# A transformer block: ScalarE takes over the copy of the k and q products, and TensorE sums the eighth key tile

## The chip, the cores and the metric

The kernel runs on one core of a Trainium2 chip. TensorE multiplies matrices, VectorE (DVE), ScalarE (ACT) and GpSimd (POOL) work on tiles element by element, SyncE (SP) issues transfers. Matmul results land in PSUM, which is divided into banks of 128 partitions by 512 fp32 elements. The metric is the device time of one execution in microseconds (us): 1811.17 us as the median of three runs of the kernel before (1810.55 to 1813.67).

## The reference

One block with conditioning, for 4 sequences of 1024 rows of 512 features, 16 heads of 32:

```python
ada = jax.nn.silu(c) @ Wada.T + bada
shift_msa, scale_msa, gate_msa, shift_mlp, scale_mlp, gate_mlp = jnp.split(ada, 6, axis=-1)
h = modulate(rmsnorm(x, g1, D), scale_msa, shift_msa)
qkv = h @ Wqkv.T + bqkv                       # -> q, k, v by head
q = rmsnorm(q, gq, hd) * hd ** (-0.5)
k = rmsnorm(k, gk, hd)
attn = jax.nn.softmax(jnp.einsum('bhqd,bhkd->bhqk', q, k), axis=-1)
o = jnp.einsum('bhqk,bhkd->bhqd', attn, v)    # -> rows of 512
x = x + gate_msa[:, None, :] * (o @ Wproj.T + bproj)
h = modulate(rmsnorm(x, g2, D), scale_mlp, shift_mlp)
x = x + gate_mlp[:, None, :] * (gelu(h @ Wfc1.T + bfc1) @ Wfc2.T + bfc2)
```

## The kernel before

The work has two parts: attention (to 977 us in the trace) and then the MLP. The change touches attention only.

**Steps.** Attention is written out as steps L = -25 to 255, and every engine has its own list of instructions in which step follows step. A step from 0 on treats one tile of 128 keys against 512 queries for a group of four heads. Eight steps (key tiles j = 0 to 7) make one half-group hh, of which there are 32; 16 steps make a group, 64 a batch b. In step L:

- TensorE (qk, L513) multiplies keys by queries into two scores banks p = 0 and 1, each holding two heads.
- ScalarE (exponentials, L704) makes two exponentials of 128x1024 from them into one of three probs buffers.
- VectorE (add, L791) adds the probs of the step before to sums, seven adds of 128x2048 for eight key tiles, since the first add takes two of them.
- TensorE (weigh, L530) multiplies probs by v. Up to step 207 it does so in odd steps for two steps at once; from then on (PAIRED = 207) one step at a time.
- One step behind the eighth key tile, TensorE sums sums over the 128 partitions (row_sums, L547: four matmuls side by side, one for each head, into the bank aux), ScalarE moves the result (move_rows, L713), and by way of DRAM its inverse comes back as a factor for the output (o_out, L801).

**Products.** Between qk(L, 0), qk(L, 1) and weigh, TensorE fills in the projections of later groups and batches: a table, PLAN, gives each product its steps (one, two or three), and six or four matmuls go into each step, half of them after qk(L, 0) and half after qk(L, 1) (fill). A product of 12 matmuls gives k or q for four heads and 512 rows (L588, called a unit) or v for 128 rows (L601). All products from step 0 on use a single bank, gemm: the first matmul of a product waits until the product before it has been moved out (bank_free). The last product ends in step 207.

**What a unit goes through.** VectorE moves it out with the bias added, into one of two raw buffers (raw_out, L816), in the step after its last. ScalarE squares it (L674), TensorE sums the squares by head into aux (sum_squares, L554), ScalarE takes the logarithm (L664) and from it, a half step later, the inverse root by an exponential (L668), both in the one buffer norms. VectorE multiplies (L862, called normalising below), splits the result into a high and a low part (L871, L873: together make_parts), and SyncE stores them to DRAM and loads them as k_stack and q_stack. The tables RAW_AT, SUM_AT, INV_AT and FIN_AT give the steps of raw_out and square, of sum_squares, of the logarithm and root, and of make_parts. SUM_AT is two steps behind the unit's end, and later where another sum, a row sum or a turn has that step; INV_AT and FIN_AT are one and two steps behind it. The logarithm of unit n waits for normalising of unit n-1 (normed) and stands ahead of its step's exponentials in ScalarE's list.

**The x tiles.** A tile of 128 rows of x for a later batch is loaded to one of three xt buffers, summed in squares (L834) and normalised (L842) by VectorE, turned by TensorE into aux (turn, L565), scaled on VectorE (L855) and split by ScalarE (L695) and GpSimd. The table TURN gives the steps, each eighth step from 50 on.

```python
RAW_AT = {step + 1: n for n, step in enumerate(UNIT_END)}
    step += 1 if step < 0 else 2                       # SUM_AT
            parts_first = L in FIN_AT and (L < 0 or L in RAW_AT and RAW_AT[L] == FIN_AT[L] + 2)
```

## Time and profile before

| | us |
|---|---|
| median of three runs | 1811.17 |
| the profiled execution's own time | 1810.62 |
| its span in the trace | 1808.8 |
| TensorE busy (matmul) | 1727.9 |
| VectorE busy | 1085.6 |
| ScalarE busy | 919.6 |
| exponentials of attention (L704), 512 | 548.7 |
| adds to sums (L791), 192 of 224 | 453.8 |
| load of an x tile, issue to landing | 3.1 |

The profile is of one execution. A busy TensorE isn't TensorE at its peak: matmuls overlap, and the ends of matmuls in the trace are modelled, so that one of 0.39 us is followed by the next 0.23 us after its start. The bracket at the end of a row is the time that the engine was idle ahead of the instruction, and what released it. Two instructions of one kind in a row are merged (x2), and a row sum of four fp32 matmuls shows as eight records. PEclk is the granted clock of TensorE as a share of 2.4 GHz.

### The profile page before, as it was taken

How to read it: one execution, taken by the hardware profiler on the slowest of the kernel's cores; microseconds unless marked ns; L12 is line 12 of the kernel's file. 1: busy time of each engine (PE TensorE's matmuls, PEld its weight loads, DVE VectorE, ACT ScalarE, POOL GpSimd, SP SyncE). 2: the span in 40 equal slices, each digit the busy share in tenths (PEclk: the TensorE clock that was granted, in tenths of full speed). 3: DMA queues.
4: the chain of work that ended last, by engine and by line, in shares of the span. 5: the costliest groups of instructions: out<-in, count | busy, mean ns of one | idle time of the engine just before them, and what ended most of it. 6: DMA issues, size and time to landing. Idle time of an engine off the chain costs nothing.

```text
span 1808.8 us, 23247 instructions
## 1 busy us (share of the span) xinstructions
PE 1727.9 (96%) x8376; PEld 1154.5 (64%) x8376; DVE 1085.6 (60%) x1325; ACT 919.6 (51%) x1136; POOL 372.5 (21%) x305
## 2 busy tenths in 40 slices
PE   6998999999999999999889999999999999999998
PEld 3554555555555555554224787878788887878786
DVE  6678888898898898878788545142332324142301
ACT  4476666777777777778787432222221212221221
POOL 3001111100001000000140233333332333333332
PEclk8999999999999999999999899999999999999999
DMA  5754545555555555555765201010020202010000
GB/s 195 214 144 132 135 123 139 132 147 135 154 135 134 146 130 156 127 135 153 174 144 196 74 18 58 25 52 24 12 70 6 64 17 64 17 52 23 17 18 24
DMA packets 122242, 176.92 MB, mean 98 GB/s; under 512 B 29568, under 2 KB 43904, under 8 KB 121136
## 3 DMA queue, kind: packets, MB, share of 16 engines
q1 hardware_dynamic: 115952, 156.41, 32.3%
q10 hardware_dynamic: 5408, 16.81, 2.5%
q0 software_dynamic: 800, 2.62, 0.5%
q8 instruction: 50, 0.82, 0.2%
q14 instruction: 32, 0.26, 0.1%
HBM read 124.87 MB, written 50.92 MB: 97 GB/s over the span
## 4 chain that ended last, share of the span: by engine, by line
PE 44%; issue 29%; DVE 11%; POOL 9%; ACT 4%; DMA 2%; SPq 0%; POOLq 0%; ACTq 0%; DVEq 0%
PE scores L513 9%; PE pv L530 8%; PE gemm L588 7%; DVE sums L791 5%; PE scores L1303 5%; POOL act_parts L1235 5%; PE gemm L601 4%; ACT probs L704 3%; PE pv L1320 3%; PE gemm L1320 2%; PE aux L554 2%; POOL y L1233 2%; PE aux L547 1%; DVE raw L816 1%; DVE raw L862 1%
## 5 line engine op out<-in xcount | busy, mean ns | idle before, releaser
L704 ACT ACTIVATE probs<-scores,shift 128x1024 f32<-128x1024 f32 x512 | 548.7, 1113 | 195.4 <-PE scores L513 178.7
L791 DVE TENSOR_TENSOR sums<-sums,probs 128x2048 f32<-128x2048 f32 x192 | 453.8, 2363 | 32.7 <-ACT probs L704 28.0
L513 PE MATMUL scores<-q_stack,k_stack 128*128 128x512 f32 x1024 | 358.8, 435 | 6.3 <-ACT probs L704 6.1
L1303 PE MATMUL scores<-w_hi,act_parts 128*128 128x512 f32 x1024 | 318.7, 392 | 0.0
L513 PEld LDWEIGHTS scores<-q_stack,k_stack 128*128 128x128 f32 x1024 | 173.8, 189 | 202.3 <-issue 105.5
L1235 POOL TENSOR_TENSOR act_parts<-act_full,act_parts 128x512 fp32r<-128x512 f32 x128 | 172.5, 1348 | 514.2 <-ACT act_parts L1166 513.6
L530 PE MATMUL pv<-probs,v 128*32 128x512 f32 x2048 | 253.1, 603 | 0.4 <-ACT probs L704 0.4
L1303 PEld LDWEIGHTS scores<-w_hi,act_parts 128*128 128x128 f32 x1024 | 191.4, 189 | 38.8
L1303 PE MATMUL scores<-w_lo,act_parts 128*128 128x512 f32 x512 | 199.9, 391 | 0.0
L1373 DVE TENSOR_TENSOR y_next<-pv,p_bias 128x512 f32<-128x512 f32 x28 | 19.3, 691 | 299.7 <-PE pv L1275 299.7
L1166 ACT ACTIVATE act_parts<-act_full 128x512 fp32r<-128x512 f32 x128 | 80.9, 632 | 224.5 <-PE scores L1303 223.5
L1320 PE MATMUL gemm<-z,w 128*128 128x512 f32 x768 | 186.9, 393 | 2.6 <-DVE z L1478 2.6
L1320 PE MATMUL pv<-z,w 128*128 128x512 f32 x768 | 185.4, 390 | 0.0
L1320 PEld LDWEIGHTS gemm<-z,w 128*128 128x128 f32 x768 | 145.7, 190 | 33.4 <-DVE z L1478 3.0
L1320 PEld LDWEIGHTS pv<-z,w 128*128 128x128 f32 x768 | 143.7, 188 | 29.8
L530 PEld LDWEIGHTS pv<-probs,v 128*32 128x32 f32 x2048 | 54.3, 110 | 133.7 <-issue 103.5
L1154 ACT ACTIVATE act_full<-gemm,f_bias 128x512 f32<-128x512 f32 x64 | 44.2, 690 | 186.4 <-PE gemm L1320 179.9
L588 PE MATMUL gemm<-h_hi,wq_hi 128*128 128x512 f32 x248 | 101.9, 411 | 22.8 <-DVE raw L816 18.9
L1154 ACT ACTIVATE act_full<-pv,f_bias 128x512 f32<-128x512 f32 x64 | 44.0, 688 | 149.2 <-PE pv L1320 147.8
L765 POOL TENSOR_TENSOR x_inv<-x_sqc,minus_half 128x1 f32<-128x1 f32 x32 | 17.6, 550 | 450.0 <-DVE x_sqc L837 450.0
L1303 PEld LDWEIGHTS scores<-w_lo,act_parts 128*128 128x128 f32 x512 | 96.6, 189 | 20.4
L588 PE MATMUL gemm<-h_hi,wq_lo 128*128 128x512 f32 x248 | 99.0, 399 | 0.0
(167 smaller groups left out, 1944.1 us busy)
## 6 DMA issues: line engine op xcount, KB each, us to landing
k_stack<-parts_scratch SPq DMA_DIRECT2D x128, 256.0 KB, 5.0
q_stack<-parts_scratch SPq DMA_DIRECT2D x128, 256.0 KB, 5.1
parts_scratch<-parts SPq DMA_DIRECT2D x62, 512.0 KB, 2.9
inverse<-inverse_scratch SPq DMA_DIRECT2D x128, 64.0 KB, 2.1
heads_out<-o_out SPq DMA_DIRECT2D x32, 256.0 KB, 5.2
out<-result SPq DMA_DIRECT2D x32, 256.0 KB, 2.0
heads<-heads_out SPq DMA_DIRECT2D x28, 256.0 KB, 3.6
x_tile<-in_x SPq DMA_DIRECT2D x28, 256.0 KB, 2.8
```

Of the source, the lines that this page charges most:

```text
L513: mm = nc.tensor.matmul(scores[p][:, i, :], k_stack[s][:, h, j * P:(j + 1) * P], q_stack[half][:, h, :], start=True, stop=True)
L530: mm = nc.tensor.matmul(pv[hh % NH][h * DH:(h + 1) * DH, :], v[b % 2][:, j, (g * HG + h) * DH:(g * HG + h + 1) * DH], probs[l % RING][:, h ...
L554: nc.tensor.matmul(aux[:], small["head_ones"][:], squares[:], start=True, stop=True).then_inc(ss_mm, 1)
L588: mm = nc.tensor.matmul(bank_of_product(p)[:], w[:, k, at:at + P], h[:, k, c], start=(n == 0), stop=(n == len(terms) - 1))
L601: mm = nc.tensor.matmul(bank_of_product(p)[:], h[:, k, c], w[:, k, 2 * D:3 * D], start=(n == 0), stop=(n == len(terms) - 1))
L704: nc.scalar.activation(probs[L % RING][:, 2 * p:2 * p + 2, :], scores[p][:], ACT.Exp, bias=small["shift"][:]).then_inc(exp_done, 1)
L791: nc.vector.tensor_tensor(sums[:], a[:], probs[l % RING][:], ALU.add).then_inc(added, 1)
L1154: nc.scalar.activation(act_full[m % 2][:], up[m % 2], ACT.Gelu_apprx_tanh, bias=f1_bias[:, m:m + 1]).then_inc(gelu_done, 1)
L1166: nc.scalar.activation(act_parts[m % 2][:, 0, :], act_full[m % 2][:], ACT.Copy).then_inc(act_hi, 1)
L1235: nc.gpsimd.tensor_tensor(act_parts[m % 2][:, 1, :], act_full[m % 2][:], full(act_parts[m % 2][:, 0, :]), ALU.subtract).then_inc(act_lo, 1)
L1303: mm = nc.tensor.matmul(acc[t], act_parts[m % 2][:, b, t * P:(t + 1) * P], w2[a][:, m, :], start=(m == 0 and i == 0), stop=(m == NM - 1 an ...
L1320: mm = nc.tensor.matmul(up[m % 2], w1[a][:, m, k, :], z[b][:, k, :], start=(k == 0 and i == 0), stop=(k == KT - 1 and i == 2))
```

## The change

Four things are done together.

1. From step 0 on, ScalarE does raw_out (an Identity activation with the bias) in the step in which the unit ends, behind the two exponentials, and squares the result at once. VectorE does it only for the four units before step 0.
2. There are three raw buffers: xt[2] becomes the third, and the x tiles of later batches have two xt buffers (XB = 2). The turns of batches 2 and 3 are a step later.
3. SUM_AT starts one step behind the unit's end, and INV_AT, FIN_AT and the loads move with it. make_parts stands behind the add in every step from 0 on.
4. From half-group 26 on (LEAN, the first that lies wholly behind the last product), VectorE leaves out the add of the eighth key tile; row_sums instead multiplies both sums and that tile's probs by ones, into the same bank.

```diff
-    TURN += [BSTEPS * b - 78 + 8 * t for t in range(NT)]
+    TURN += [BSTEPS * b - 77 + 8 * t for t in range(NT)]
...
-RAW_AT = {step + 1: n for n, step in enumerate(UNIT_END)}
+RAW_AT = {step + (1 if step < 0 else 0): n for n, step in enumerate(UNIT_END)}
...
-    step += 1 if step < 0 else 2
+    step += 1
...
+LEAN = -(-max(FILL) // NT)
+
+def adds_until(l):
+    hh, j = l // NT, l % NT
+    return ADDS * min(hh, LEAN) + (ADDS - 1) * max(0, hh - LEAN) + (min(j, ADDS - 1) if hh >= LEAN else j)
...
+    def raw_of(n):
+        return raw[n % 2] if n < 4 else (raw + [xt[XB]])[n % 3]
...
         def row_sums(hh):
-            pe.wait_ge(added, ADDS * (hh + 1))
+            pe.wait_ge(added, adds_until(NT * hh + NT - 1))
             aux_free()
             for h in range(HG):
-                mm = nc.tensor.matmul(aux[h * DH:(h + 1) * DH, :], small["ones"][:], sums[:, h, :], start=True, stop=True)
+                mm = nc.tensor.matmul(aux[h * DH:(h + 1) * DH, :], small["ones"][:], sums[:, h, :], start=True, stop=(hh < LEAN))
+            if hh >= LEAN:
+                l = NT * hh + NT - 1
+                pe.wait_ge(exp_done, 2 * l + 2)
+                for h in range(HG):
+                    mm = nc.tensor.matmul(aux[h * DH:(h + 1) * DH, :], small["ones"][:], probs[l % RING][:, h, :], start=False, stop=True)
...
+        def raw_out(n):                                        # ScalarE
+            act.wait_ge(unit_mm, n + 1)
+            act.wait_ge(part_lo, max(4, n - 2))
+            nc.scalar.activation(raw_of(n)[:], bank_of_product(PRODUCT_OF_UNIT[n])[:], ACT.Identity, bias=qk_bias[:, col:col + 1]).then_inc(raw_done, 1)
...
             if L >= 0:
                 exponentials(L, 0)
                 exponentials(L, 1)
+            if L >= 0 and L in RAW_AT:
+                raw_out(RAW_AT[L])
+                square(RAW_AT[L])
...
-            if j == 0:
+            if j == 0 or hh >= LEAN and j == NT - 1:           # VectorE's add
                 return
...
-            parts_first = L in FIN_AT and (L < 0 or L in RAW_AT and RAW_AT[L] == FIN_AT[L] + 2)
+            parts_first = L in FIN_AT and L < 0
...
-            if L in RAW_AT:
+            if L < 0 and L in RAW_AT:
                 raw_out(RAW_AT[L])
```

ScalarE's list in steps 10 to 12, before. A row ending in x2 is one step's pair of exponentials; raw and xt hold units, squares and norms are as named above.

```order
L704 ACTIVATE probs_71<-scores,shift 128x1024 x2
L664 ACTIVATE norms<-aux,ln_floor 128x512
L704 ACTIVATE probs_72<-scores,shift 128x1024 x2
L668 ACTIVATE norms<-norms,ln_bias 128x512
L674 ACTIVATE squares<-raw_54 128x512
L704 ACTIVATE probs_70<-scores,shift 128x1024 x2
```

And after, for the same three steps:

```order
L734 ACTIVATE probs_71<-scores,shift 128x1024 x2
L696 ACTIVATE raw_54<-gemm,qk_bias 128x512
L702 ACTIVATE squares<-raw_54 128x512
L684 ACTIVATE norms<-aux,ln_floor 128x512
L734 ACTIVATE probs_72<-scores,shift 128x1024 x2
L688 ACTIVATE norms<-norms,ln_bias 128x512
L684 ACTIVATE norms<-aux,ln_floor 128x512
L734 ACTIVATE probs_70<-scores,shift 128x1024 x2
L696 ACTIVATE xt_60<-gemm,qk_bias 128x512
L702 ACTIVATE squares<-xt_60 128x512
```

The copy and the square stand behind the exponentials of steps 10 and 12, and the logarithms of two units now stand in steps 11 and 12, with one pair of exponentials between them.

TensorE's list in steps 154 and 155, before. Unit 50 ends with the second pair of L588 rows; L565 is the turn of an x tile.

```order
L513 MATMUL scores<-q_stack_67,k_stack_65 128x512 x2
L588 MATMUL gemm<-h_lo,wq_hi 128x512
L588 MATMUL gemm<-h_hi,wq_lo 128x512
L565 MATMUL aux<-ident,xt_60 128x128 x4
L513 MATMUL scores<-q_stack_67,k_stack_65 128x512 x2
L588 MATMUL gemm<-h_hi,wq_hi 128x512
L588 MATMUL gemm<-h_lo,wq_hi 128x512
L513 MATMUL scores<-q_stack_67,k_stack_65 128x512 x2
L588 MATMUL gemm<-h_hi,wq_lo 128x512
L588 MATMUL gemm<-h_hi,wq_hi 128x512
L530 MATMUL pv<-probs_70,v_68 32x512 x4
```

And after:

```order
L527 MATMUL scores<-q_stack_67,k_stack_65 128x512 x2
L608 MATMUL gemm<-h_lo,wq_hi 128x512
L608 MATMUL gemm<-h_hi,wq_lo 128x512
L527 MATMUL scores<-q_stack_67,k_stack_65 128x512 x2
L608 MATMUL gemm<-h_hi,wq_hi 128x512
L608 MATMUL gemm<-h_lo,wq_hi 128x512
L527 MATMUL scores<-q_stack_67,k_stack_65 128x512 x2
L608 MATMUL gemm<-h_hi,wq_lo 128x512
L608 MATMUL gemm<-h_hi,wq_hi 128x512
L585 MATMUL aux<-ident,xt_59 128x128 x4
L544 MATMUL pv<-probs_70,v_68 32x512 x4
```

The turn has moved from ahead of the next unit's first matmul (L588, L608: gemm<-h_hi,wq_hi) to behind its fourth.

TensorE's list around the row sum of half-group 26 (step 217), before:

```order
L513 MATMUL scores<-q_stack_67,k_stack_65 128x512 x4
L547 MATMUL aux<-sums,ones 32x512 x4
L530 MATMUL pv<-probs_70,v_69 32x512 x4
L513 MATMUL scores<-q_stack_67,k_stack_65 128x512 x4
L530 MATMUL pv<-probs_71,v_69 32x512 x4
```

And after, where the L567 row reads the eighth key tile:

```order
L527 MATMUL scores<-q_stack_67,k_stack_65 128x512 x4
L561 MATMUL aux<-sums,ones 32x512 x4
L567 MATMUL aux<-probs_72,ones 32x512 x4
L544 MATMUL pv<-probs_70,v_69 32x512 x4
L527 MATMUL scores<-q_stack_67,k_stack_65 128x512 x4
L544 MATMUL pv<-probs_71,v_69 32x512 x4
```

A second set of four matmuls follows the first.

## Rows read from the trace of the kernel before

**Rows 1.** The page, part 1: busy us (share), xinstructions.

```profile
PE 1727.9 (96%) x8376; PEld 1154.5 (64%) x8376; DVE 1085.6 (60%) x1325; ACT 919.6 (51%) x1136; POOL 372.5 (21%) x305
```

**Rows 2.** Busy by stretch: us; PE, PEld, DVE, ACT, POOL; PEclk, DMA, GB/s.

```profile
69.60:399.70 330.10, 310.34 (x1584) 177.83 (x1583) 272.24 (x304) 231.83 (x263) 32.44 (x24) 0.98 0.52 136
399.70:848.20 448.50, 439.24 (x2354) 241.89 (x2352) 393.36 (x388) 341.48 (x384) 28.09 (x24) 1.00 0.54 140
848.20:977.30 129.10, 117.27 (x624) 39.00 (x622) 107.77 (x60) 108.18 (x110) 26.78 (x19) 0.97 0.56 139
...
132.10:208.80 76.70, 68.51 (x340) 39.74 (x339) 66.75 (x91) 50.06 (x58) 9.45 (x9) 0.96 0.54 148
```

**Rows 3.** Groups by line, 120 to 1050 us: busy, mean ns, idle before.

```profile
L791 DVE TENSOR_TENSOR sums<-sums,probs 128x2048 f32<-128x2048 f32 x184 | 435.5, 2367 | 30.6 <-ACT probs L704 25.9
...
L816 DVE TENSOR_SCALAR raw<-gemm,qk_bias 128x512 f32<-128x512 f32 x55 | 41.2, 748 | 16.2 <-PE gemm L588 15.2 <-issue 0.3
L664 ACT ACTIVATE norms<-aux,ln_floor 128x512 f32<-128x512 f32 x56 | 38.6, 689 | 17.3 <-PE aux L554 10.7 <-DVE raw L862 6.2
...
L674 ACT ACTIVATE squares<-raw 128x512 f32<-128x512 f32 x56 | 35.0, 625 | 1.1 <-PE aux L554 1.1
L713 ACT ACTIVATE inverse<-aux 128x512 f32<-128x512 f32 x31 | 18.7, 603 | 17.0 <-PE aux L547 17.0
```

**Rows 4.** TensorE's waits in stretch A: total us, times, longest.

```profile
PE gemm L588 <- DVE raw L816: 13.7, 13, 2.6
PE gemm L588 <- DVE v L826: 3.9, 4, 2.0
PE gemm L601 <- DVE raw L816: 1.5, 3, 0.6
```

**Rows 5.** The same for stretch B.

```profile
PE gemm L588 <- DVE raw L816: 5.2, 10, 0.7
...
PE gemm L601 <- DVE raw L816: 1.8, 4, 1.2
```

**Rows 6.** Timeline about step 20's end: start, us, engine line, [idle <-releaser].

```profile
149.71 2.20 ACT L704 ACTIVATE probs<-scores,shift 128x1024 f32<-128x1024 f32 x2 [1.49 <-PE scores L513]
...
153.19 0.75 DVE L816 TENSOR_SCALAR raw<-gemm,qk_bias 128x512 f32<-128x512 f32 x1
...
154.00 0.50 PE L588 MATMUL gemm<-h_hi,wq_hi 128*128 128x512 f32 x1 [1.22 <-DVE raw L816]
```

**Rows 7.** Timeline about step 132's end.

```profile
584.30 2.12 ACT L704 ACTIVATE probs<-scores,shift 128x1024 f32<-128x1024 f32 x2 [1.37 <-PE scores L513]
...
586.42 0.50 PE L601 MATMUL gemm<-wq_hi,h_hi 128*128 128x512 f32 x1 [0.22 <-DVE raw L816]
```

**Rows 8.** Timeline about step 154's end, with the turn of an x tile.

```profile
661.81 2.12 ACT L704 ACTIVATE probs<-scores,shift 128x1024 f32<-128x1024 f32 x2 [1.64 <-PE scores L513]
...
662.92 0.60 PE L565 MATMUL aux<-ident,xt 128*128 128x128 f32 x4
663.27 0.71 PE L513 MATMUL scores<-q_stack,k_stack 128*128 128x512 f32 x2
...
664.64 0.50 PE L588 MATMUL gemm<-h_hi,wq_hi 128*128 128x512 f32 x1 [0.66 <-DVE raw L816]
```

**Rows 9.** Timeline of steps 149 and 150: the logarithm's wait and TensorE's.

```profile
644.51 0.69 ACT L664 ACTIVATE norms<-aux,ln_floor 128x512 f32<-128x512 f32 x1 [2.41 <-DVE raw L862]
...
646.25 0.73 PE L513 MATMUL scores<-q_stack,k_stack 128*128 128x512 f32 x2 [1.06 <-ACT probs L704]
```

**Rows 10.** TensorE's waits in stretch C.

```profile
PE aux L547 <- DVE sums L791: 7.3, 3, 3.5
```

**Rows 11.** Timeline of row sums in stretch C, steps 217 and 225.

```profile
875.08 1.72 PE L547 MATMUL aux<-sums,ones 128*32 128x512 f32 x8 [3.45 <-DVE sums L791]
...
896.32 1.07 PE L547 MATMUL aux<-sums,ones 128*32 128x512 f32 x8
...
897.21 1.04 PE L530 MATMUL pv<-probs,v 128*32 128x512 f32 x8
```

More of the change, by code:

```diff
@@ L51 @@
 XS = 3
+XB = 2
 AFTER = B * BSTEPS
@@ L123 @@
 HOUT_AT = {step: n for n, step in enumerate(HOUT) if n not in HOUT_ACT.values()}
-XLOAD_AT = {step + 1: n + XS for n, step in enumerate(TURN) if NT <= n < B * NT - XS}
-XLOAD_AT.update({NT + n: NT + n for n in range(XS)})
+XLOAD_AT = {step + 1: n + XB for n, step in enumerate(TURN) if NT <= n < B * NT - XB}
+XLOAD_AT.update({NT + n: NT + n for n in range(XB)})
 SPLIT_W = {"act": {-23: 0, -20: 1, -17: 2}, "dve": {-20: 0, -19: 1, -16: 2}}
@@ L362, in x_of @@
     def x_of(n):
-        return xt[n % XS] if n < XS or n >= NT else mem["x_ahead"][n - XS]
+        return xt[n % XB] if n >= NT else xt[n] if n < XS else mem["x_ahead"][n - XS]
     x_ahead_in = [sem(f"x_ahead_in{n}") for n in range(NT)]
@@ L370, in x_landed @@
             return x_ahead_in[n], 16
-        return x_in[n % XS], 16 * sum(1 for m in range(NT, n + 1) if m % XS == n % XS)
+        return x_in[n % XB], 16 * ((n - NT) // XB + 1)
+    def raw_of(n):
+        return raw[n % 2] if n < 4 else (raw + [xt[XB]])[n % 3]
     def parts_of(n):
@@ L396, in load_x @@
             if n >= NT:
-                sp.wait_ge(turned, n - XS + 1)
+                sp.wait_ge(turned, n - XB + 1)
             b, t = n // NT, n % NT
@@ L668, in inverse_root @@
             nc.scalar.activation(norms[:], norms[:], ACT.Exp, scale=-0.5, bias=small["ln_bias"][:]).then_inc(norm_done, 1)
+        def raw_out(n):
+            b, g, which, half = UNIT[n]
+            col = (0 if which == "q" else NG) + g
+            act.wait_ge(unit_mm, n + 1)
+            act.wait_ge(part_lo, max(4, n - 2))
+            nc.scalar.activation(raw_of(n)[:], bank_of_product(PRODUCT_OF_UNIT[n])[:], ACT.Identity, bias=qk_bias[:, col:col + 1]).then_inc(raw_done, 1)
         def square(n):
@@ L673, in square @@
                 act.wait_ge(ss_mm, n)
-            nc.scalar.activation(squares[:], raw[n % 2][:], ACT.Square).then_inc(sq_done, 1)
+            nc.scalar.activation(squares[:], raw_of(n)[:], ACT.Square).then_inc(sq_done, 1)
         def first_h_out(n):
@@ L701, in exponentials @@
                 act.wait_ge(pv_mm, l + 1)
-                act.wait_ge(added, ADDS * (l // NT) + max(1, l % NT))
+                act.wait_ge(added, adds_until(l + 1 if l % NT == 0 else l))
+                if l // NT >= LEAN and l % NT == NT - 1:
+                    act.wait_ge(rs_mm, l // NT + 1)
             act.wait_ge(qk_mm, 2 * L + p + 1)
@@ L788, in add @@
             else:
-                dve.wait_ge(added, hh * ADDS + j - 1)
+                dve.wait_ge(added, adds_until(l - 1))
                 a = sums
@@ L815, in raw_out @@
                 dve.wait_ge(part_lo, n - 1)
-            nc.vector.tensor_scalar(raw[n % 2][:], bank_of_product(PRODUCT_OF_UNIT[n])[:], qk_bias[:, col:col + 1], None, ALU.add).then_inc(raw_done, 1)
+            nc.vector.tensor_scalar(raw_of(n)[:], bank_of_product(PRODUCT_OF_UNIT[n])[:], qk_bias[:, col:col + 1], None, ALU.add).then_inc(raw_done, 1)
         def v_out(n):
@@ L859, in make_parts @@
         def make_parts(n):
-            r = raw[n % 2]
+            r = raw_of(n)
             dve.wait_ge(norm_done, n + 1)
@@ L876, in vector @@
         for L in range(START, AFTER):
-            parts_first = L in FIN_AT and (L < 0 or L in RAW_AT and RAW_AT[L] == FIN_AT[L] + 2)
+            parts_first = L in FIN_AT and L < 0
             if parts_first:
                 make_parts(FIN_AT[L])
-            if L in RAW_AT:
+            if L < 0 and L in RAW_AT:
                 raw_out(RAW_AT[L])
```

## The prediction

> **What bounds the kernel now.** I read the page for shares, then the table by stretches, since the change lies only in the attention part, steps 0 to 255. [rows 1] shows TensorE at 96% of the span, VectorE at 60%. [rows 2] cuts attention into three stretches: steps 0 to 79 (A, 69.6 to 399.7 us), steps 80 to 207 (B, to 848.2) and steps 208 to 255 (C, to 977.3). In A VectorE is busy 272.2 of 330.1 us and at its densest, steps 16 to 31, 66.75 of 76.7 us, while TensorE's clock is 0.96. In B TensorE is busy 439 of 448.5 us: it is the bound. In C no products are left and TensorE, ScalarE and VectorE hand over to each other at about the same pace.
>
> The waits say what TensorE lacks. In A it waits 13.7 + 1.5 us, in 16 waits, for VectorE's move of a k or q product out of the projection bank, and 3.9 us for v products [rows 4]. A printed wait is short by some 0.17 us, because a matmul's modelled end hides it, so the k and q moves cost about 15.2 + 16 x 0.17 = 18 us. In B the same waits are 5.2 + 1.8 us [rows 5].
>
> **The moved copy.** VectorE gives up 60 copies of 0.748 us; ScalarE takes 60 that the trace doesn't show. The nearest rows of ScalarE reading a 128x512 bank are 0.603 (inverse<-aux) and 0.689 us (norms<-aux, which also has a bias by partition) [rows 3]. I take 0.69, keeping 0.60 to 0.75. The square (0.625) only moves forward. By the Trainium skill (VectorE: DVE Perf Modes, section The TRN2 errata — SBUF-src ops pay a fixed extra latency per instruction) ScalarE from PSUM takes 172 cycles plus one per element at 1.2 GHz, an estimate of 0.57 us for 512; the trace's 0.603 and 0.689 are above it, and with 0.57 the sum below would end some 3 us lower.
>
> What matters is when the bank comes free. Now the copy stands behind both exponentials of the step that ends the product. I went through all 60 ends: new time free = end of the second exponential + 0.69 + 0.03; old time free = end of VectorE's copy.
>
> Stretch A. At step 20 the exponentials end at 149.71 + 2.20 = 151.91, so the bank would be free at 152.63, where VectorE, behind three other pieces, starts only at 153.19 and TensorE goes on at 154.00 [rows 6]: 1.4 us regained. Of the 28 ends in A, eleven keep a sum-of-squares matmul in the same step as cover (left over: about 0), eight are left with part of their cover (about 0.5 us each), six have none (0.9 to 1.2 each) and three end in odd steps, where two steps' pv products, about 1 us each [rows 11], hide everything. That leaves 10 us of the 18: minus 8. VectorE limits this: without copies it still has 66.75 - 6 x 0.75 = 62.3 us of work in steps 16 to 31, with its own waits not counted. I charge 1 us for that and give 1 us for v products that it now moves sooner. The low clock: 76.7 us at 0.96 is 3.1 us lost in two falls [rows 2], 1.5 each; A's 0.98 over 330.1 us is four such falls, three of them right after the longest waits for a copy (up to 2.6 us [rows 4]). These three go: minus 4.5.
>
> Against it stands a wait that the new table makes. The logarithm of product n waits until VectorE has normalised product n-1, since both use norms, and it stands in front of the next exponentials. Where two sums of squares are in neighbouring steps this blocks ScalarE: at 644.51 it has waited 2.41 us, and TensorE then 1.06 us for the exponential [rows 9]. Before, there are three such pairs; now five in A (second logarithms in steps 12, 38, 44, 54, 70) and none in B. I take 1.1 us each: plus 5.5. The lower end is 0.65, where no product ends in that step; the upper is add + normalise, about 3 us. The Trainium skill (PSUM — Partial Sum Buffer, section Engine vs sequencer instructions) calls ScalarE's queue strictly first in, first out. [rows 9] agrees: exponentials whose scores were ready stood behind the logarithm.
>
> A = -8 + 0 - 4.5 + 5.5 = -7 us.
>
> Stretch B. Here VectorE was mostly prompt, and ScalarE is later. At 585 the exponentials end at 584.30 + 2.12 = 586.42; adding 0.72 gives 587.14, but TensorE goes on at 586.42 today [rows 7]: six such ends, 0.75 each, plus 4.5. With an x tile's turn in the step, the exponentials end at 661.81 + 2.12 = 663.93, so the bank is free at 664.65 against 664.64 now [rows 8]; but the turn, 0.35 us of TensorE that filled this wait (662.92 to 663.27), now comes a step later, where nothing waits: seven ends, 0.39 each, plus 2.7. Two ends with a turn where VectorE was prompt lose both, 1.1 each, plus 2.2. One end gains 0.3. Two of the old logarithm waits go, 2 x 1.06, minus 2.1. Odd ends cost nothing. B = +7 us.
>
> Stretch C. Row sums wait 7.3 us for VectorE's adds [rows 10]. Leaving out one add of 2.37 us [rows 3] in seven takes away all of it. Two of the waits, 3.45 us at 875.08 for one, drop the clock: the eight row-sum matmuls take 1.72 instead of 1.07 us [rows 11]; C's clock of 0.97 over 129.1 us [rows 2] is 3 to 4 us for the two falls, I take 3.4. In exchange each of six row sums does its set of matmuls twice, 897.21 - 896.32 = 0.89 us each [rows 11], plus 5.3, on the path, since these groups already run at TensorE's hand-over. Another 0.5 goes behind the last step, where VectorE is free earlier. C = -7.3 - 3.4 + 5.3 - 0.5 = about -6 us.
>
> Two x buffers instead of three cost nothing: a tile loads two turns ahead, 16 steps in B, and at the tightest place (load in step 20, used in 22) still two steps, 9.6 us, of which the transfer (3.1 us to land) needs a third. The third raw buffer only loosens the wait for the parts of two products back, which is never last here. The part after attention is untouched.
>
> **Sum.** -7 + 7 - 6 = -6 us on the profiled execution's 1810.6, 1804.6; the median shown is 0.55 above that execution, so 1805.
>
> **Rivals.** (1) No change, chance 0.24. VectorE stays the bound of A's dense steps, where it has 87% of the time, and the new logarithm waits take what is left, so A brings 0: 0 + 7 - 6 = +1, 1812. For it: the 62.3 us of work that stay there are strung on waits of their own. Against it: the longest waits stand exactly behind copies. (2) A larger gain, 0.15. All four falls and the v waits (3.9) go, logarithm waits cost 0.65 and the copy 0.60, which makes A about -16, and B loses only 5: 1811 - 16 + 5 - 6 = 1794; I give it as 1799, half of that extra. (3) Slower, 0.13. The logarithm wait grows: ScalarE has 7.6 us per two steps in the dense part (4.25 exponentials, copy 0.69, square 0.63, logarithm and root 1.4, high part 0.62) against the 76.7 / 8 = 9.6 that two steps take now and the 8.6 that I expect, so a blocked 3 us is not made up before the next product; five places at 3.05 instead of 1.1, and two new falls of the clock at 1.5, are +12.7: A = +6, total +7, 1818. It decides from 3 us a place. For it: [rows 9] stands in a stretch where ScalarE has far more slack, and the wait reached TensorE even there. Against it: the score products run a step ahead. (4) The change does not do what it says, 0.03: the bank copy on ScalarE is no shorter than VectorE's 0.75 and its place behind the exponentials costs at every end; then A = -3: 1809.
>
> **How the numbers follow.** The forecast's own case has 0.45 and spans 1801 to 1809. About 0.2% (3.6 us) is what a measurement of this kernel can tell from none, so faster means below 1807.5 and slower above 1814.8. Faster: most of the forecast's case (0.40), all of rival 2 and a part of 1, together 0.61. Same: the rest of the forecast, most of rivals 1 and 4, 0.25. Slower: rival 3 and a tail of 1, 0.14. The range for 8 in 10 is 1796.5 to 1814.
>
> **What would show it.** TensorE's waits for the bank in A down from 15.2 us to 7 or 8, now for ScalarE, and in B up from 7 to 11 or more; the copy's row near 0.69 us; a logarithm waiting for VectorE five times in A; PEclk of 1.0 in A save one fall, and in C throughout; no wait of a row sum for an add in C. Stretch lengths: A 323, B 455, C 123 us. I am wrong if B does not grow, if A shrinks by less than 3, or if a row sum's second set costs nothing.

## The result, and the profile after

The changed kernel takes 1819.91 us (median of 7 runs, 1818.66 to 1824.02), the kernel before beside it 1812.5 us (7 runs, 1808.37 to 1814.01): ratio 1.0045, 95% interval 1.003 to 1.006. It is slower by 0.45%, where 1805 was forecast, and outside the forecast's range. The profiled execution took 1823.64 us, 3.7 above the median, with a span of 1821.8.

The page's busy lines answer to [rows 1]: the copies have moved from VectorE to ScalarE.

```profile
PE 1736.7 (95%) x8424; PEld 1156.4 (63%) x8424; DVE 1023.8 (56%) x1259; ACT 954.0 (52%) x1196; POOL 373.7 (21%) x305
```

The same table by stretches as in [rows 2] (A, B and C; columns as there):

```profile
72.05:405.45 333.40, 310.95 (x1584) 176.12 (x1583) 253.03 (x277) 246.34 (x291) 25.83 (x24) 0.98 0.50 131
405.45:862.44 456.99, 441.90 (x2354) 242.65 (x2352) 366.27 (x357) 361.63 (x416) 32.24 (x24) 1.00 0.55 138
862.44:989.97 127.53, 120.01 (x662) 40.53 (x662) 94.49 (x53) 107.99 (x110) 30.67 (x19) 0.97 0.61 146
```

Against before, A is 3.3 us longer (330.1 to 333.4; forecast 7 shorter), B 8.5 longer (forecast 7 longer), C 1.5 shorter (forecast 6 shorter). PEclk is 0.98 in A and 0.97 in C, as before, where the forecast had one fall left in A and none in C. What lies before attention has the same instructions in all kernels here and took 69.5 to 73.0 us, by where the clock falls.

One group of the lines of instructions, 40 of ScalarE's 60 copies (min/median/max in ns, first and last start):

```profile
L696 ACT ACTIVATE raw<-gemm,qk_bias x40: 676/687/707, 89.2 to 861.2; 128x512 f32<-128x512 f32 x40
```

TensorE's waits in A answer to [rows 4] (total us, times, longest):

```profile
PE gemm L608 <- ACT raw L696: 6.2, 9, 0.8
PE scores L527 <- ACT probs L734: 4.9, 5, 1.2
PE aux L585 <- DVE xt L875: 3.4, 1, 3.4
PE gemm L608 <- DVE v L859: 2.7, 4, 1.8
PE gemm L621 <- DVE v L859: 2.1, 3, 1.5
PE gemm L621 <- ACT raw L696: 1.7, 2, 0.9
PE gemm L608 <- ACT xt L696: 1.5, 2, 0.9
```

and those in B to [rows 5]:

```profile
PE gemm L608 <- ACT raw L696: 5.9, 7, 0.8
PE gemm L608 <- ACT xt L696: 4.2, 5, 0.8
PE gemm L621 <- ACT raw L696: 2.5, 3, 0.8
PE gemm L608 <- DVE v L859: 1.3, 4, 0.3
PE gemm L621 <- ACT xt L696: 0.8, 1, 0.8
```

In A the waits for copies fell from 15.2 to 9.4 us. Beside them stand two new kinds: five waits, 4.9 us, for exponentials behind a logarithm (steps 12, 38, 44, 54 and 70, the five pairs foreseen), and one of 3.4 us for a turn. The waits for v products, 4.8 us in seven, are hardly changed: before, they were 4.6 in six, since a fourth row belongs to [rows 4]:

```profile
PE gemm L601 <- DVE v L826: 0.7, 2, 0.4
```

In B the waits for copies rose from 7.0 to 13.4.

A foreseen wait, in step 12 (timeline: start, us, engine, line; in brackets the idle time before and its releaser). The second logarithm of two neighbouring sums waits for VectorE; the exponentials behind it come late, then also the copy of the product that ends in this step:

```profile
121.41 0.69 ACT L684 ACTIVATE norms<-aux,ln_floor 128x512 f32<-128x512 f32 x1 [2.41 <-DVE raw L895]
123.16 0.73 PE L527 MATMUL scores<-q_stack,k_stack 128*128 128x512 f32 x2 [0.67 <-ACT probs L734]
124.74 0.50 PE L608 MATMUL gemm<-h_hi,wq_hi 128*128 128x512 f32 x1 [0.85 <-ACT xt L696]
```

The one not foreseen, in step 23: VectorE's list runs without a gap through add, parts and statistics, and the tile that TensorE is to turn is normalised last.

```profile
166.67 0.68 DVE L895 SCALAR_TENSOR_TENSOR xt<-norms,xt 128x512 f32<-128x512 f32 x1
...
168.58 0.68 DVE L867 CUSTOM_DVE_ANT_0 unused<-xt 128x512 f32<-128x512 f32 x1
...
170.12 1.48 DVE L875 TENSOR_SCALAR xt<-xt,x_inv,x_gain 128x512 f32<-128x512 f32 x1 [0.66 <-POOL x_inv L798]
171.66 1.11 PE L585 MATMUL aux<-ident,xt 128*128 128x128 f32 x4 [3.38 <-DVE xt L875]
```

The turn's four transposes take 1.11 us, where e6 below has 0.66 for the same: the clock fell during this wait (granted clock 0.50 from 170.8 to 177.6 us, the 1.2 GHz level).

In C no row sum waits for an add any more. But step 224 starts late (TensorE, GpSimd's loads, SyncE's transfers, same columns):

```profile
875.88 0.95 POOL L1213 DMA_DIRECT2D y<-heads_out  x1 [135.34 <-issue]
892.70 0.76 POOL L1213 DMA_DIRECT2D y<-heads_out  x1 [6.32 <-issue]
893.33 1.80 SPq L443 DMA_DIRECT2D q_stack<-parts_scratch  x4
896.36 0.34 SPq L460 DMA_DIRECT2D inverse_scratch<-compact  x1
905.69 1.71 SPq L465 DMA_DIRECT2D inverse<-inverse_scratch  x4
905.59 2.05 PE L527 MATMUL scores<-q_stack,k_stack 128*128 128x512 f32 x4 [3.00 <-issue]
```

GpSimd issues four loads of 256 KB for the part after attention from 892.70 on, and the loads of the q products of step 224 (from 893.33) go out among them. The median time to landing of these four q loads is 8.8 us here, where it was 4.9 before; the last of them lands at 905.5, and step 224 starts at 905.59. An 8 KB transfer issued at 896.36 releases its successor only at 905.69, just behind them. The clock then falls (PEclk 0.50 from 904.7 to 911.5 us).

```profile
q_stack<-parts_scratch SPq DMA_DIRECT2D x4, 256.0 KB, 8.8
```

### The profile page after: what moved, and what is told of

Read it like the earlier page. It is cut to its first block, busy times and chain, and to the rows that moved or that the text cites. A ratio compares the mean times of both kernels' runs of the same rounds, so it can differ in the third digit from the quotient of the medians.

```text
span 1821.8 us, 23336 instructions
## 1 busy us (share of the span) xinstructions
PE 1736.7 (95%) x8424; PEld 1156.4 (63%) x8424; DVE 1023.8 (56%) x1259; ACT 954.0 (52%) x1196; POOL 373.7 (21%) x305
## 4 chain that ended last, share of the span: by engine, by line
PE 49%; issue 28%; POOL 8%; ACT 8%; DVE 5%; DMA 1%; POOLq 0%; ACTq 0%; SPq 0%; DVEq 0%
PE scores L527 10%; PE pv L544 9%; PE gemm L608 7%; ACT probs L734 6%; PE scores L1336 5%; POOL act_parts L1268 5%; PE gemm L621 4%; DVE sums L824 3%; PE aux L574 3%; PE pv L1353 3%; PE gemm L1353 2%; PE aux L561 2%; POOL y L1266 2%; POOL z L1253 1%; DMA wstage<-in_wqkvT 1%
## 5 line engine op out<-in xcount | busy, mean ns | idle before, releaser
L824 DVE TENSOR_TENSOR sums<-sums,probs 128x2048 f32<-128x2048 f32 x186 | 432.1, 2323 | 80.9 <-ACT probs L734 78.7
L608 PE MATMUL gemm<-h_hi,wq_hi 128*128 128x512 f32 x248 | 101.5, 409 | 21.8 <-ACT raw L696 12.1
L824 DVE TENSOR_TENSOR sums<-probs,probs 128x2048 f32<-128x2048 f32 x32 | 73.4, 2292 | 63.8 <-PE aux L561 39.3
```

The source lines that it names most:

```text
L608: mm = nc.tensor.matmul(bank_of_product(p)[:], w[:, k, at:at + P], h[:, k, c], start=(n == 0), stop=(n == len(terms) - 1))
L824: nc.vector.tensor_tensor(sums[:], a[:], probs[l % RING][:], ALU.add).then_inc(added, 1)
```

## The experiments

All stretches below are measured from the first exponential of steps 0, 80 and 208 to the end of the last. The medians of before beside these runs were 1810.25 to 1812.74 us.

| run | what it is | median us | ratio to before, interval | A | B | C |
|---|---|---|---|---|---|---|
| before | | 1812.5 | | 330.1 | 448.5 | 129.1 |
| after | | 1819.91 | 1.0045, 1.003-1.006 | 333.4 | 457.0 | 127.5 |
| e1 | before + eighth tile | 1803.92 | 0.9952, 0.9936-0.9969 | 326.3 | 448.6 | 122.4 |
| e2 | after, without eighth tile | 1826.35 | 1.0068, 1.0053-1.0084 | 333.7 | 456.8 | 133.8 |
| e3 | after, no neighbouring sums | 1811.11 | 0.999, 0.9978-1.0002 | 324.1 | 457.0 | 124.9 |
| e4 | after, turns as before | 1817.95 | 1.0034, 1.0021-1.0047 | 332.8 | 455.2 | 125.6 |
| e5 | after, sums as before | 1804.44 | 0.9957, 0.9944-0.9971 | 323.2 | 455.4 | 122.3 |
| e6 | covering sums, ScalarE copies | 1798.21 | 0.9928, 0.9914-0.9941 | 320.6 | 451.0 | 122.4 |
| e7 | the same, VectorE copies | 1805.79 | 0.9972, 0.996-0.9984 | 324.0 | 456.5 | 122.6 |
| e8 | the same, mixed | 1804.42 | 0.9965, 0.9951-0.9979 | 320.1 | 456.3 | 122.6 |
| e9 | sums, turns, squares as before | 1804.64 | 0.9957, 0.994-0.9974 | 320.9 | 457.9 | 122.4 |
| e10 | e6, tiles normalised earlier | 1794.96 | 0.9909, 0.9893-0.9925 | 317.0 | 451.9 | 122.3 |
| e11 | e10, eighth tile in 5 more heads | 1799.1 | 0.9929, 0.9913-0.9945 | 321.8 | 451.6 | 122.3 |
| e12 | the best of each | 1783.9 | 0.9846, 0.9828-0.9863 | 315.6 | 441.4 | 122.6 |
| e13 | after, loads later in the program | 1819.66 | 1.0046, 1.003-1.0061 | 333.5 | 457.1 | 128.2 |
| e14 | after, tiles normalised earlier | 1819.83 | 1.0045, 1.0029-1.006 | 333.2 | 456.9 | 126.6 |
| e15 | after, last sum as before | 1817.43 | 1.0039, 1.0026-1.0051 | 331.0 | 457.1 | 122.8 |

B repeats within 0.3 us between kernels that are alike there; A does not, since the clock falls at other places in each execution (before and e1 have the same instructions in A, as have after, e2, e13 and e15: 331.0 to 333.7). Read from the traces' granted clock, a fall in A loses 1.7 us, or 3.4 where it lasts twice as long. A loses 6.8 us so in before, after, e2, e13 and e14, 3.4 in e1, e4, e5, e6, e8, e9, e11 and e15, and 1.7 in e3, e7, e10 and e12. A difference in A must be read with this beside it.

**e1, one part alone.** Before with `LEAN`, `adds_until` and the second set of `row_sums` as in the change.

> The kernel before, with nothing changed but the eighth key tile of the last six heads' row sums on TensorE (the copies, the sums of squares and the turns stay as they were). Stretches A (steps 0 to 79) and B (80 to 207) should be those of before, 330 and 448.5 us. For C (208 to 255, 129.05 us before) the theory, from the changed kernel's trace: the waits of the row sums for the adds (7.3 us) and the two clock falls behind them go, the second sets cost about 0.9 each, which is C at 123; but the loads for step 224 now come late, so that the scores of that step wait some 5 us, as at 905.59 us of the changed kernel: C 127 to 128, the whole -1.5 (ratio 0.999). Rival: that wait has to do with the moved copies' table (which also brings GpSimd's loads two steps forward) and is not there: C 123, the whole -6 (ratio 0.9967).

C is 122.4: the eighth tile is worth 6.7 us, near the forecast's 6, and there is no wait at step 224. The rival came true, not the theory: that wait comes with the change's other parts.

**e2, the other part alone.** `LEAN = NC * NG` in the changed kernel.

> The changed kernel with the eighth key tile back on VectorE for all heads: only the copies on ScalarE, the earlier sums of squares, the turns one step later and the raw buffer remain of the change. Theory, that the two parts add up: A 333.5 and B 457 us as in the changed kernel, C 129 as before, so +11.8 on the trace's stretches and about +9 to +11 on the median of before (ratio 1.0055). Rival, that the difference in A is the luck of single clock falls: A 330, the whole +8 (ratio 1.0045).

The parts add up in A and B. C is 4.7 longer than before although no row sum changed, which I had not expected: the q loads of step 224 land late here too, and the clock falls more often (0.95 in C, 0.97 before).

**e3, the neighbouring sums.**

```diff
-    while step in SUM_AT or step in ROWS_AT or step in TURN_AT and step >= 0:
+    while step in SUM_AT or step in ROWS_AT or step >= 0 and (step in TURN_AT or step - 1 in SUM_AT):
```

> The changed kernel with one rule added: no sum of squares in the step right after another one. Five pairs fall apart, eight of the 64 sums move one step later, nothing else. Theory, that the second logarithm of a pair (2.41 us of ScalarE waiting for VectorE's normalising) costs TensorE what its waits in these steps add up to, 8.7 us, and one clock fall with it: A from 333.4 to about 324, the whole 1811. Rival 1, my forecast's price of 1.1 us each: A 328, the whole 1814.5. Rival 2, that VectorE's own list bounds these steps: A no more than 2 us shorter.

A is 9.3 shorter and the whole 1811, the theory's numbers, but not by its sum. 5.1 us are the clock (PEclk 0.995 for 0.980 in A). TensorE's printed waits in A fell only from 22.4 to 19.1 us: the logarithms' 4.9 went, the copies' fell from 9.4 to 5.5, because sums that move a step later also come to lie behind a product's end, and the waits for v products rose from 4.8 to 9.7. Steps 8 to 15, where the change has one of its pairs and neither run a clock fall, take 31.1 for 34.8 us.

**e4, the turns.** `BSTEPS * b - 77` back to `- 78`.

> The changed kernel with the turns of the third and fourth images one step earlier again, where before had them: in the last step of a product. Theory, that a turn there fills TensorE's wait for ScalarE's copy: seven ends get back 0.39 us and two more up to 1.1, B from 457.0 to 453 to 454; A within 1 us (its pairs of sums change from 68/69 to 51/52). The whole about -3. Rival, that the turn's normalise and the statistics in VectorE's list matter more, being a step nearer to the copy's old place: B unchanged.

B is 1.8 shorter, a step block with a turn (8 steps) 28.25 for 28.48 us: 0.23 per turn, where I had 0.39 and more; B was expected at 453 to 454 and is 455.2.

**e5, the sums two steps behind their product.**

```diff
-    step += 1
+    step += 1 if step < 0 else 2
     while step in SUM_AT or ...
```

> The changed kernel with each sum of squares two steps behind its product's end again, as before had them, where the change has them one step behind; the copies stay on ScalarE, the turns one step late. New theory, which the forecast lacked: a copy's wait is hidden by whatever TensorE has to do behind the product in the same even step, a sum of squares (0.9 us) above all, and the earlier table took this cover away from eleven even ends of A (6, 8, 12, 14, 16, 38, 44, 54, 56, 70, 76) and eight of B, v products among them, and made the five pairs of sums. With the cover back, 0.85 us for each k or q end and 0.33 for each v end: A about 318 (7.8 by cover, 6 by the pairs' logarithms, 1.5 by a clock fall), B about 452.3. The loads that hang on the last sum come two steps later too, so C as in the eighth tile alone, 122.4. The whole about 1796 (ratio 0.991). Rival 1, that VectorE's list bounds A: A not under 324, as with the sums apart. Rival 2, that the wait at step 224 belongs to the copies on ScalarE and not to the two steps: C 125 to 127.

A 10.2, B 1.6 and C 5.2 us shorter: the earlier sums alone cost the change some 15 us on the median. Rival 2 fails. The theory's 318 for A and 1796 for the whole fail too, and rival 1 misses by less than a clock fall (323.2 for its 324). Of A's 10.2, 3.4 are the clock. The logarithms' waits went and the copies' fell from 9.4 to 3.6 us, but those for v products rose from 4.8 to 9.5: nearly half of the saving went into waits for VectorE.

**e6 to e8, cover by rule.** A sum goes into the first step, two or more behind its product's end, in which another product ends; turns as before but one.

```diff
+    covering = [s for s in range(end + 2, following + 1) if end >= 0 and s in ENDS and not taken(s)]
+    step = covering[0] if covering else end + 1
```

e6 copies all on ScalarE (`ON_ACT`: `end >= 0`), e7 none, e8 those of `6 <= end < 56`.

> All copies on ScalarE, and each sum of squares put, by rule, into the step in which the next product ends (k, q or v), the turns where before had them but one: uncovered even ends of k and q products fall to 4, 32, 40, 48, 124, 178, 188, with a turn (0.35 us) as cover at ten. Cover theory: against the sums two steps behind, B loses another 4.4 us, to 448, the value of before with copies on VectorE, A 317.5, C 122.4, the whole about 1791 (ratio 0.988). Rival, that ScalarE's copy costs at every even end what it did because it lengthens ScalarE's own list: B 452 or more.

> The same table of sums and turns, and the eighth key tile on TensorE, but all copies on VectorE in the step behind the product, as before the change. This tells what the copies on ScalarE are worth by themselves when cover is the same. Cover theory: an uncovered even end costs 0.42 here, B falls from 448.5 to about 446.8 (132, 140, 196, 204 covered), A stays 326 to 330, since in steps 8 to 55 VectorE's late copies are the wait, C 122.4: the whole about 1801 (ratio 0.9935). Rival, that cover hides the late copies of A as well: A 318 as on ScalarE, the whole 1792.

> The same table again, with copies on ScalarE only for products that end in steps 6 to 55, where VectorE is late, and on VectorE elsewhere. If both theories hold (cover by the table, lateness of VectorE in the dense part alone) it takes the better half of each: A about 316, B 446.8, C 122.4, the whole about 1788 (ratio 0.987), faster than either kernel. Rival, that the two arrangements are equal once the cover is there: same as with all copies on ScalarE within 1 us.

e6 is the first version faster than all before it, though 7 us short of its theory. In A ScalarE's copies are worth 3.4 us over VectorE's with equal cover (320.6, 324.0; e8, with ScalarE's in the dense part, has 320.1), and not by the clock, which is lower in e6 (0.989, 0.995). In B the blocks with turns are equal (28.22 and 28.30 us for 8 steps). e7 and e8 missed in B by 9.7 and 9.5 us: my rule put the sums of the products ending in steps 76 and 79 into steps 79 and 80. The second is one step behind its product, and with VectorE's copies that product is copied and squared only in step 80, so TensorE stands until ScalarE's square is done:

```profile
397.06 1.13 PE L585 MATMUL aux<-squares,head_ones 128*128 128x512 f32 x2 [2.03 <-ACT squares L713]
```

A clock fall follows in step 80. Steps 80 to 87 are 3.8 us longer than before, those from 144 to 151, with the same wait of 2.03 and no fall, 2.4. In e6 the square of the product ending in step 79 is done in that step, and the wait is not there.

**e9, the engine alone.** `raw_out` on ScalarE in the product's last step, with the tables of sums and turns as before and squares a step behind. The eighth tile, the three raw buffers and the place of `make_parts` are those of the change.

> What the move of the copy to ScalarE is worth by itself: the changed kernel with the sums of squares two steps behind the product, the turns and the squares all where before had them; against the run with the eighth tile alone only the engine (and step) of the 60 copies, with its raw buffer, differs. Cover theory: in A the dense part (steps 8 to 55) gains what VectorE was late, A 320 to 322 against 326.3; in B the seven uncovered even ends (124, 132, 140, 178, 188, 196, 204) lose 0.43 each and the ends with a turn nothing, B 451.5 against 448.6; C 122.4. The whole about 1801, so the copy on ScalarE by itself is a gain of some 2 us and the loss of the change is its tables'. Rival, my forecast's: every even end of B without a sum loses 0.39 to 0.75, B 455, the whole 1805, no gain.

A is 5.4 us shorter than in e1 at the same clock (0.99), B 9.3 longer, the median the same (1804.64 and 1803.92). So the move of the copies itself brings nothing in sum, as the rival had it: 1805, where I expected 1801. The turns' waits come with this part of the change and not with the tables: TensorE waits 3.8 us for two turns here (steps 21 and 23), and for none before. Six of B's 9.3 are at the two old pairs of sums, where the copy now queues too, and a clock fall follows each:

```profile
410.39 0.69 ACT L684 ACTIVATE norms<-aux,ln_floor 128x512 f32<-128x512 f32 x1 [2.41 <-DVE raw L896]
412.14 0.73 PE L527 MATMUL scores<-q_stack,k_stack 128*128 128x512 f32 x2 [1.09 <-ACT probs L734]
413.72 0.50 PE L621 MATMUL gemm<-wq_hi,h_hi 128*128 128x512 f32 x1 [0.85 <-ACT raw L696]
```

**e10, e11, e14: what binds the dense part.** The first and third have

```diff
-STAT += [step - 1 for step in TURN[NT:]]
-NORM += TURN[NT:]
+STAT += [step - 2 for step in TURN[NT:]]
+NORM += [step - 1 for step in TURN[NT:]]
```

on e6 and on the changed kernel; e11 adds heads 1 to 5 to `LEAN`.

> All copies on ScalarE with the covering table, and the statistics and the normalising of the x tiles one step earlier. In that table's trace TensorE's turns still wait 1.4 and 2.4 us for the normalised tile (steps 21 and 23), which stands at the end of VectorE's unbroken list, with a clock fall behind the longer one. Theory: moving them forward takes both waits and that fall, 5 us: steps 16 to 31 from 74.7 to about 70, A from 320.6 to about 315.5, the whole from 1798.2 to 1793. Rival 1, VectorE is full there and the delay only moves to the parts and the v products (1.8 and 1.4 us now): steps 16 to 31 not under 73. Rival 2: the x tile itself lands too late, and VectorE stands: slower.

> The same, and the eighth key tile on TensorE for heads 1 to 5 as well (steps 8 to 47), which takes 2.3 us from VectorE in each and gives TensorE 0.87. Theory, that VectorE's sheer work bounds steps 16 to 31: the waits for v products (1.8 and 1.4) and their clock fall go too, 4.7 us for 1.7 of TensorE's there, while heads 4 and 5 (and 1), where VectorE has slack, lose 0.87 each: A about equal, 314.5 to 316. Rival, that it is only the order of VectorE's list: nothing gained, A longer by 5 times 0.87, 4.4 us.

> The changed kernel with only the statistics and normalising of the x tiles one step earlier. Theory, that in steps 16 to 31 TensorE is bound by the order of VectorE's list, with the normalised tile last in it: the turn's wait of 3.4 us and the clock falls behind it go, steps 16 to 31 from 75.3 to about 70, and a little in B (up to 0.4 per 8 steps where a copy stood behind the normalising): A 328, the whole about 1813. Rival, that the neighbouring sums' logarithms take it over: steps 16 to 31 not under 74.

The turn's wait goes in both, and in the changed kernel A still takes 333.2: steps 16 to 31 lose 3.0 us, steps 32 to 55 take 2.9 back. There the longest waits of TensorE over steps 16 to 47 now are

```profile
PE scores L527 <- ACT probs L734: 3.7, 2, 2.6
PE gemm L608 <- DVE v L859: 3.2, 1, 3.2
```

where they were 1.9 (longest 1.2) and 2.0 (longest 1.8). So neither the theory (A 328) nor the rival (steps 16 to 31 not under 74) holds. In e10, without neighbouring sums, it is mainly the v product's wait that grows (in step 31 from 1.8 to 3.2), and 3.6 us stay, 1.7 of them clock. e11 took 3.9 us of VectorE's work out of steps 16 to 31. Stretch 16 to 31 of e10 (first) and e11:

```profile
130.80:201.84 71.04, 65.95 (x340) 38.64 (x339) 62.79 (x85) 52.94 (x64) 12.89 (x9) 0.98 0.59 161
```

```profile
133.40:205.06 71.66, 67.62 (x356) 39.35 (x355) 58.89 (x83) 53.01 (x64) 12.25 (x9) 0.98 0.57 156
```

It gained nothing: with 1.7 us more of TensorE's work the stretch is 0.6 longer, A as a whole 4.8 (the rival said 4.4), and the longest wait is the same 3.2 us for a v product. So what binds here is in the main the order of VectorE's list; of its amount, 3.9 us less can have brought 1.1 at most.

**e13 and e15: step 224.** e13 sets `TAIL = max(FIN_AT) + 3`, e15 puts one sum back, that of the last product, from step 208 to 210.

> The changed kernel with only the loads for the part after attention (GpSimd's of heads, bias and x, counted from the last sum of squares) two steps later, where before had them. Theory, that these loads fill the DMA queues just when the last row sums' small transfers and the stack loads want them, so that SyncE comes late to the loads of step 224: C from 127.5 to 122.4, A and B as in the changed kernel (333.4, 457.0), the whole about 1814.5. Rival, that it is the last parts' store and the stack loads themselves, two steps earlier too: C stays at 125 to 127.5.

> The changed kernel with only the last of the 64 sums of squares moved, from step 208 to 210, where before had it. GpSimd's loads for the part after attention wait until the last product's parts are stored, because they overwrite those buffers; in the changed kernel they start 13.4 us after step 208 begins, in the runs without the stall 19 to 19.6 us after. Theory, that these loads, released too early, crowd out SyncE's small transfers and the loads for step 224: C from 127.5 to 122.4, A and B as in the changed kernel, the whole about 1814.5. Rival, that the other sums' places (the parts of products 61 and 62 one step earlier) make the crowd: C 125 or more.

e13 changed nothing: GpSimd still issued its first load 13.4 us after step 208 began. The step in which a load is written does not hold it back; by the code the first load waits until the last product's parts are stored. e15 moves it to 20.1 us after, and the stall is gone:

```profile
877.93 0.95 POOL L1213 DMA_DIRECT2D y<-heads_out  x1 [142.04 <-issue]
...
892.29 0.76 POOL L1213 DMA_DIRECT2D y<-heads_out  x1 [3.31 <-issue]
```

```profile
888.94 1.80 SPq L443 DMA_DIRECT2D q_stack<-parts_scratch  x4
892.21 0.34 SPq L460 DMA_DIRECT2D inverse_scratch<-compact  x1
897.45 1.71 SPq L465 DMA_DIRECT2D inverse<-inverse_scratch  x4
```

GpSimd's bunch of four loads now starts 3.4 us behind the load of the q products, not 0.6 ahead; the q loads land in 5.6 us (median) in place of 8.8, and the 8 KB transfer releases its successor after 5.2 us in place of 9.3. C is 122.8, but the median fell by 2.5 us only: the stall's price differs between executions, and with the same last sum, and the tile on TensorE, C is 124.9 (e3) to 128.2 (e13).

Is it GpSimd's loads, or the parts' store and the stack loads, which moved too? The traces of all kernels speak for GpSimd's. In the six whose last sum is in step 208 (after, e2, e3, e4, e13, e14), three of the four loads of the bunch are issued 30.6 to 32.8 us after step 208 began, and the last q load lands at 42.6 to 44.3. In the eleven others the same three are issued at 34.1 to 37.2, and it lands at 38.1 to 39.4. The q loads themselves are issued at about the same time in both (29.2 to 33.2), long after the last parts' store (9.7 or 15 us). No run moves GpSimd's loads alone. By the Trainium skill (DMA: Bandwidth & Descriptors, section Queues, rings and completion order) a transfer's semaphore write lands only after all earlier writes of its DMA engine, in whatever queue. The 8 KB transfer agrees, in landing 0.2 us behind the last q load in both runs, but no run here looks at single DMA engines.

**e12, the best of each.** ScalarE's copies and covering sums for products ending in steps 6 to 55, VectorE's copies and sums two steps behind from 56 on (covering again from 188), none neighbouring, tiles normalised a step earlier.

> The version that the runs so far point to: copies on ScalarE with covering sums for products ending in steps 6 to 55, copies on VectorE with the table of before from step 56 on (covering sums again from 188), no two sums in neighbouring steps, x tiles normalised a step earlier, the eighth tile on TensorE at the end. By stretches already measured: A 314.5, B 447.3 (448.5 less 0.6 in steps 192 to 199 and less the two pairs of sums), C 122.5: with 70 to 73 before and 832 behind, about 1789 (ratio 0.988). Rival, that the earlier statistics cost VectorE's prompt copies in B: B 450, the whole 1792.

1783.9 us, 1.5% faster than before, 2% than the change. B is 6 us better than expected: TensorE has no wait at all in steps 96 to 103. Before, VectorE's add and with it the copy of the step's product stood behind a normalising that waits for GpSimd (0.66 us); normalised a step earlier, the copy is prompt (27.35 us for 28.07). This is read from the two traces; no run has it alone.

```profile
70.63:386.18 315.55, 303.66 (x1584) 174.89 (x1583) 257.55 (x283) 242.22 (x283) 33.14 (x24) 0.99 0.54 141
386.18:827.58 441.40, 438.63 (x2354) 241.76 (x2352) 392.33 (x389) 340.95 (x383) 30.11 (x24) 1.00 0.56 143
```

## Why the prediction was wrong

In sum the change is three things: the eighth tile, a gain of 0.5% (e1); the copy's engine, nothing (e9 against e1, -5.4 in A and +9.3 in B); and the tables of sums, squares and turns that came with it, a loss of some 15 us on the median (after against e9), 12.5 in A and 5.2 in C, with 0.9 given back in B. Of A's 12.5, 3.4 are the clock; in e15's execution, at e9's clock, it is 10.1. The forecast gave the tables only the logarithms' 5.5, the cover that A's copies lose, and the turns' part of B.

**A, forecast -7, measured +3.3: the step that failed is the clock term, -4.5, with VectorE's, where 1 us charged stood against 1 us given.**
- Copies, forecast -8: waits from 15.2 in 16 to 9.4 in 13; with 0.17 for each, 17.9 to 11.6, so -6.3. (Twelve of the ends keep a sum in their step by the table, not eleven.) The copy took 0.687 us, as assumed. The rule of the Trainium skill (VectorE: DVE Perf Modes, section The TRN2 errata — SBUF-src ops pay a fixed extra latency per instruction) gave 0.57 as an estimate; the trace stands above it.
- Logarithms, forecast +5.5: five waits, 4.9 printed and 0.17 each, +5.7. Right. In the rows at 121.41 and 123.16 nothing overtook the waiting logarithm. That agrees with what the Trainium skill says of ScalarE's queue (PSUM — Partial Sum Buffer, section Engine vs sequencer instructions).
- VectorE, forecast 0 in sum: a turn waits 3.4 us where none did, and the v waits did not shrink (4.8 in seven for 4.6 in six): +3.9. I had added up VectorE's work without copies (62.3 us; it is 61.7) and compared it with the time; but what TensorE waits for is the last item of an unbroken list, and it now arrived before that item. e14 shows that taking this wait away alone gives nothing back; e11, that less work does little either.
- Clock, forecast -4.5: the granted clock is 0.98 over A before and after, 6.8 us lost in both, so 0. The three waits for copies behind which it was to stop falling did shrink or go, and others took their part: the turn's 3.4 in step 23, where it lasted twice as long, and a logarithm with a copy in step 44; the fall behind a v product in step 31 stayed. Nor is this one execution's luck. Over all executions of the whole kernel the mean granted clock is 0.987 before and 0.989 after, some 23 and 21 us lost; 7.9 were to come back in A and C together.

The four make +3.3. Rival 1, that VectorE stays the bound of the dense steps, described A; it had 0.24 and no cost for C. Rival 3 had nearly the number (1818) and not the reason: the logarithms cost 1.1 us a place, not 3.

**B, forecast +7, measured +8.5: right in direction and size, in part by luck.** The mechanism holds: waits of 0.65 to 0.85 at even ends where there were 0.4 or none, +0.4 in each block of 8 steps with a turn, +0.8 to 1.4 in the six blocks with other uncovered ends, -0.7 in the two blocks where an old pair of sums stood. But the turns, forecast 4.9, gave back 1.8 in e4; the sums a step earlier, for which B had no term, 1.6 in e5; if these add up, the rest is 5.1 where 2.1 was forecast. e9 shows that the old pairs left in place would have made it worse.

**C, forecast -6, measured -1.5: the terms were right, one was missing, and put at nothing by the sentence that the part after attention is untouched.** e1 has -6.7 with the same row sums. The forecast counted only TensorE, ScalarE and VectorE in C. But the last sum of squares came two steps earlier, with it the last parts' store, and with that GpSimd's loads, which then ran beside the q loads of step 224. Putting that sum back takes 4.7 us off C in the profiled executions (e15) and 2.5 off the median; in the changed kernel's profile it is a wait of 3.0 us with 3.4 of clock behind it. Whom a moved step releases was asked for B and not for the last product.

What stays open: which of GpSimd's loads delays the q loads (queue and engine of each were not separated), and why the move of the copies makes two turns wait.

## What to carry to other kernels

Moving a copy to another engine can gain where the old engine is late and lose as much where it was prompt; here it came to nothing. What also counts is which work of the waiting engine lies behind the product's end and hides the copy. Keep that work there when the copy moves, and put no two users of one single buffer into neighbouring steps. An engine at 80 to 87% whose list has no gap can bind by its order: ask which item is last and who waits for it, and expect the next item to be waited for when that one is moved. When the last instance of something moves forward, follow what it releases, also on queues that no step paces.

## What the runs showed of the hardware

- The clock's falls differ between executions of the same instructions: A took 330.1 and 326.3 us with before's code, 331.0 to 333.7 with the change's. A wait of 2.4 us for a turn in step 23 was followed by a fall in e6 (granted clock 0.96 in steps 16 to 23) and by none in e3 (1.00). So a forecast that single falls go is worth no more than their size, up or down: 1.7 us each here, 3.4 for a long one.
- The time of a transfer depends on what else is issued: loads of 256 KB landed in 4.9 us (before), 5.6 (e15) or 8.8 (after, beside four others), and the same 8 KB release took 3.5, 5.2 or 9.3 us in these three.
- ScalarE's copy of a 128x512 bank with a bias by partition took 0.687 us, VectorE's 0.748.
